# First expert layer on tokens sorted by expert, with rows gathered by index and outputs gathered back per token

## The chip, the cores and the metric

The kernel is one program on one core of a Trainium2 chip. The metric is device time in microseconds of one execution, the median of a few runs. The engines are PE (TensorE; PEld is its weight load), DVE (VectorE), ACT (ScalarE), POOL (GpSimd) and SP (SyncE, which issues the transfers of the kernel before; SPq is its queue).

## What is computed

Four layers follow each other on x, 8 batches of 256 tokens with 128 features. Each layer is a cross-attention and a feed-forward part, both on the layer-normed x and both added to x. The feed-forward part of the first layer is a channel mix; those of the other three are mixtures of eight experts. The change is in the second layer's, `moe1` in the kernel:

```python
logits = xf @ router_w.T                       # xf: 2048 tokens x 128, eight experts
routing = softmax(logits)
top_w, top_i = top_k(routing, 2); top_w = top_w / sum(top_w)
combine = zeros(N, E).at[arange(N)[:, None], top_i].add(top_w)
g = einsum('nd,ehd->neh', xf, w_gate)          # hidden size 256
u = einsum('nd,ehd->neh', xf, w_up)
y = einsum('neh,edh->ned', silu(g) * u, w_down)
out = einsum('ned,ne->nd', y, combine)
```

Only two of eight entries of a row of `combine` are not zero.

## The kernel before, in words

x stays in SBUF as `x_sb`, 16 tiles of 128 tokens by 128 features. The program is written out per engine; engines meet through semaphores that count named events. `EVENTS` lists them; `wait` and `done` turn a stage, block and step into a count. Each engine runs its own list in order.

The stages are, in order, `att0` with `ffn0` and `att1` (one flow of 16 steps), `moe1`, `att2`, `moe2`, `att3`, `moe3`. An attention flow goes in steps of one batch, and each step in beats of one head; in a step, the scores' rows of one batch (maxima on DVE, L712), the exponentials of the batch before (ACT, L1256) and the output of the batch before that are interleaved. After the last batch come steps with `tail` 0 to 3, in which less and less is left of the attention; the statistics, norms and transposes (`stats_all`, `apply_all`, `turn_all`) of the next stage stand there, at fixed beats.

In `moe1` each of four blocks of 512 tokens goes through each of eight experts (`block_of`, `down`, `add_y`). For one block and one expert PE makes four products of 512 columns from the transposed tokens `zt` (gate and up, two halves of the hidden size each, L1810). A float32 product is two passes on PE. ACT takes Silu of the gate (`gated`, L1407), DVE multiplies it by up (`ht`, L971). PE then makes eight products of 128 columns with the down weights (L1778), and DVE adds each of the four 128-token results to `x_sb` with the router's weight as a scalar (`add_y`, L950); the weight is zero for six of eight experts. Blocks 1 and 2 are a loop with a register; blocks 0 and 3 are written out. Beside block 0 the router runs on DVE (`route_logits`, `route_pick`, `route_weights`). Beside the last block the first step of the next attention, `att2`, runs (`beside_last_block`, `EARLY_BEATS`). The router looks at its tokens in two groups, `GROUPS`, of 12 and 4 tiles.

All weights of the layer are one transfer into `pack_moe`, made at the start. `stack` are three buffers that hold the attention's keys and queries, split into bf16 parts; `scratch` is a DRAM table that `moe3` uses. Nothing in the kernel before is addressed by data, and POOL issues no transfer.

## Time and profile before

| | |
|---|---|
| three runs, median (lowest to highest) | 907.48 us (905.09 to 909.58) |
| profiled execution, its own time | 905.37 us |
| its span, from the first to the last instruction | 903.6 us |
| mean granted TensorE clock | 0.96 |
| instructions | 14923 |
| DMA moved | 44.52 MB |

The span is what the profile shows; 1.8 us of the profiled execution's time lie around it. Times of rows are microseconds from the start of the span unless marked ns. PEclk in a window is the granted clock of TensorE as a share of full speed: 1.00 is 2.4 GHz, 0.50 is 1.2 GHz.

### The profile page before, as it was taken

Reading aid. Unit: us, or ns where it says so; the run is one execution under the profiler, and the core shown is the slowest. Engines: PE = TensorE matmul, PEld = TensorE weight load, DVE = VectorE, ACT = ScalarE, POOL = GpSimd, SP = SyncE. Lnnn points to the kernel's source line nnn. Section 1 sums busy time; section 2 is a strip of 40 time slices with the busy share of each in tenths; the row PEclk is TensorE's granted clock in tenths of the full one; section 3 lists DMA queues with packets and bytes.
Section 4 is the critical chain, followed back from the end, with each engine's and each line's share of the span. In section 5 each row is a group of like instructions: output and inputs, shape, how many; then the busy total and the mean of one; then the engine's idle time right before and its main releaser. Section 6 shows DMA issues by size and latency. Waiting matters only on the chain. (4 is left out here: it accounts for less than half of the span.)

```text
span 903.6 us, 14923 instructions
## 1 busy us (share of the span) xinstructions
PE 787.9 (87%) x5120; PEld 533.7 (59%) x5120; DVE 513.8 (57%) x1423; ACT 391.6 (43%) x764; POOL 174.6 (19%) x316
## 2 busy tenths in 40 slices
PE   1687888999988899999997897789999887769998
PEld 1355666666655566666665565467777666546665
DVE  4577768767775374444556775484235434445453
ACT  2565554566667532222222665453333455232221
POOL 4444455333301000000013442200001001000000
PEclk9999999999999999999997999899999999569999
DMA  9422212321110000000014331000000200023332
GB/s 308 115 69 66 71 55 61 88 68 55 55 55 2 1 1 1 1 0 0 1 36 138 89 84 38 1 1 1 1 0 1 79 1 1 1 72 95 94 95 68
DMA packets 55277, 44.52 MB, mean 49 GB/s; under 512 B 5048, under 2 KB 50104, under 8 KB 54728
## 3 DMA queue, kind: packets, MB, share of 16 engines
q1 hardware_dynamic: 55208, 43.63, 16.5%
q8 instruction: 39, 0.64, 0.3%
q14 instruction: 30, 0.25, 0.1%
HBM read 20.09 MB, written 1.11 MB: 23 GB/s over the span
## 5 line engine op out<-in xcount | busy, mean ns | idle before, releaser
L712 DVE TENSOR_REDUCE negmax<-ps 128x2 f32<-128x512 f32 x256 | 170.0, 687 | 88.2 <-PE ps L1539 87.2
L1256 ACT ACTIVATE exps<-ps 128x512 f32<-128x512 f32 x256 | 148.2, 598 | 79.8 <-PE ps L1551 78.3
L1810 PE MATMUL ps<-zt,pack_moe 128*128 128x512 f32 (+1 forms) x384 | 177.5, 598 | 0.9 <-DVE ht L971 0.9
L1778 PEld LDWEIGHTS ps<-pack_moe,ht 128*128 128x128 f32 x1024 | 124.0, 192 | 30.7 <-issue 28.8
L1778 PE MATMUL ps<-pack_moe,ht 128*128 128x128 f32 x1024 | 124.6, 275 | 0.5 <-ACT ht L1410 0.5
L950 DVE SCALAR_TENSOR_TENSOR x_sb<-ps,weights,x_sb 128x128 f32<-128x128 f32 (+1 forms) x256 | 72.1, 344 | 79.7 <-PE ps L1778 79.5
L1539 PE MATMUL ps<-stack 96*128 96x256 bf16 x512 | 100.4, 290 | 19.2 <-DVE negmax L712 14.1
L1551 PE MATMUL ps<-stack 99*128 99x256 bf16 x512 | 98.1, 281 | 14.9 <-DMA stack<-maxt 10.1
L1810 PEld LDWEIGHTS ps<-zt,pack_moe 128*128 128x128 f32 x384 | 68.9, 193 | 63.7 <-issue 62.1
L1407 ACT ACTIVATE gated<-ps 128x512 f32<-128x512 f32 x64 | 38.1, 597 | 117.1 <-PE ps L1810 117.0
L971 DVE TENSOR_TENSOR ht<-ps,gated 128x512 f32<-128x512 f32 x64 | 44.0, 691 | 57.9 <-ACT gated L1407 57.8
L1551 PEld LDWEIGHTS ps<-stack 99*128 99x128 bf16 x512 | 43.4, 100 | 54.1 <-DMA stack<-maxt 20.4
L1539 PEld LDWEIGHTS ps<-stack 96*128 96x128 bf16 x512 | 47.2, 101 | 41.7 <-DVE negmax L712 28.1
L1567 PE MATMUL ps<-exps,values 128*32 128x256 f32 x1024 | 69.8, 388 | 0.5 <-ACT exps L1256 0.5
L1410 ACT ACTIVATE ht<-ps,pack_moe 128x512 f32<-128x512 f32 x64 | 43.2, 686 | 57.6 <-PE ps L1810 56.3
L1425 ACT ACTIVATE gated<-ps 128x512 f32<-128x512 f32 x36 | 21.5, 597 | 77.5 <-PE ps L1842 77.4
L1853 PEld LDWEIGHTS ps<-pack_moe,ht 128*128 128x128 f32 x288 | 37.6, 193 | 19.8 <-issue 13.5
L940 DVE TENSOR_TENSOR ht<-ps,gated 128x512 f32<-128x512 f32 x36 | 24.9, 691 | 39.6 <-ACT gated L1425 39.5
L1069 POOL TENSOR_SCALAR var_eps<-moments 128x2 f32<-128x2 f32 x24 | 4.7, 197 | 208.1 <-DVE moments L594 202.7
L1853 PE MATMUL ps<-pack_moe,ht 128*128 128x128 f32 x288 | 38.7, 277 | 2.7 <-DVE ht L940 2.7
L1567 PEld LDWEIGHTS ps<-exps,values 128*32 128x32 f32 x1024 | 28.7, 110 | 19.4 <-issue 6.4
L1840 PE MATMUL ps<-stack,pack_moe 128*128 128x512 f32 x64 | 33.9, 611 | 5.3 <-DVE stack L1010 5.3
(183 smaller groups left out, 1053.8 us busy)
## 6 DMA issues: line engine op xcount, KB each, us to landing
stack<-qk_parts SPq DMA_DIRECT2D x168, 128.0 KB
stack<-weights_t SPq DMA_DIRECT2D x32, 256.0 KB, 3.2
pack_moe<-in_moe SPq DMA_DIRECT2D x1, 3076.0 KB, 14.6
pack_moe<-in_moe SPq DMA_DIRECT2D x1, 2129.0 KB, 9.6
pack_moe<-in_moe SPq DMA_DIRECT2D x1, 1732.0 KB, 7.0
out<-x_sb SPq DMA_DIRECT2D x4, 256.0 KB, 2.3
x_sb<-in_x SPq DMA_DIRECT2D x1, 896.0 KB, 6.0
ctxt_sb<-in_ctxt SPq DMA_DIRECT2D x1, 768.0 KB, 8.0
```

The lines of the kernel that those rows point to most:

```text
L712: dve.tensor_reduce(negmax_of[b % 2][:, :, h:h + 1].rearrange("p t h -> p (t h)"), ps[:, h % 2, :].rearrange("p (t k) -> p t k", t=2), AX, ...
L950: last = dve.scalar_tensor_tensor(out=xt, in0=ps[:, 4 + e % 2, t * D:(t + 1) * D], scalar=w, in1=xt, op0=ALU.mult, op1=ALU.add)
L971: dve.tensor_tensor(ht[:, e % 2, c, :], ps[:, 2 * c + 1, :], gated[:, c, :], ALU.mult)\
L1256: nc.scalar.activation(exps[:, i, :], ps[:, 2 + h % 2, :], ACT.Exp, scale=scale)\
L1407: nc.scalar.activation(gated[:, c, :], ps[:, 2 * c, :], ACT.Silu).then_inc(sem["gate_done"], 1)
L1410: nc.scalar.activation(ht[:, e % 2, c, :], ps[:, 2 * (e % 2) + c, :], ACT.Gelu, bias=par(s, "b1")[:, k:k + 1]).then_inc(sem["h_ready"], 1)
L1539: last = pe.matmul(ps[:, h % 2, t * T:(t + 1) * T], st[0:MAXROW, h, 0, t * P:(t + 1) * P], st[0:MAXROW, h, 1, :], start=True, stop=True)
L1551: last = pe.matmul(ps[:, 2 + h % 2, t * T:(t + 1) * T], st[0:MAXROW + 3, h, 1, t * P:(t + 1) * P], st[0:MAXROW + 3, h, 0, :], start=True, ...
L1567: last = pe.matmul(ps[STRIP * k:STRIP * (k + 1), AV, r * T:(r + 1) * T], values[nh][:, buf(s, a), kt, u, :], exps[:, slot(s, a, u), kt * T ...
L1778: last = pe.matmul(ps[:, 4 + e % 2, t * D:(t + 1) * D], ht[:, e % 2, c, t * P:(t + 1) * P], par(s, "wd" if s == "moe1" else "w2")[:, k * P ...
L1810: last = pe.matmul(ps[:, bank, :], par(s, name)[:, k * P:(k + 1) * P], zt[:, bass.ds(2 * blk, 2), 1:1 + T], start=True, stop=True)
L1853: last = pe.matmul(ps[:, 4 + blk % 2, t * D:(t + 1) * D], ht[:, q % 2, 0, t * P:(t + 1) * P], par(s, "w2")[:, w * P:(w + 1) * P], start=(q ...
```

## The change

The tokens are taken in two halves of 1024 (`HALVES`). In each half the two picks of every token are put in order of expert, each expert's rows padded up to whole tiles of 128. 8 experts and 2048 rows need at most 23 tiles (`TILES`), so 46 tiles are always computed (`ALL_TILES`). The steps for one half:

- The normed rows go to a DRAM table (`store_table`, on SP).
- `rank_tokens` (PE) counts, with triangular and all-ones matrices, how many picks of each expert stand ahead of each token. `place_tokens` (DVE) makes the row of each pick from it. `make_lists` (DVE) writes one-hot matrices, `list_tokens` (PE) multiplies them into the token number of each row, and `read_tokens` (DVE) makes integers of them. `make_lists` also makes the expert of each tile as an offset into the weights.
- POOL gathers 128 rows per tile by indirect DMA (`fetch_rows`), six tiles ahead (`AHEAD`).
- PE turns the rows, multiplies them by gate and up weights at the offset read into a register (one product of 512 columns with the rows as weights), turns the hidden values (two transposes) and multiplies them by the down weights. ACT copies the turned rows and hidden values out of PSUM and takes Silu; DVE multiplies, and copies the output to `y_kept`.
- SP stores each output tile to DRAM (`store_output`).
- POOL fetches, for each token tile, the rows of its two picks (`fetch_output`), and DVE adds them to `x_sb` with the shares as scalars (`join_outputs`).

The first half's routing stands in the steps `tail` -1 to 2 of `att1` (`SORT_STEPS`), the second half's beside the tiles 1 to 20 (`SORT_BEATS`). The first half's outputs are fetched from loop step 26 on, the second half's in the steps of `att2`. The first batch of `att2` runs beside tiles 33 to 45 (`EARLY_TILES`).

```diff
-    "moe1": [("router", 8), ("wg", 2048), ("wu", 2048), ("wd", 2048)],
+    "moe1": [("router", 8), ("experts", 6144)],
+TOKENS = 1024
+PARTS = 2
+TILES = E + (2 * TOKENS - E) // P
+ALL_TILES = PARTS * TILES
+AHEAD = 6
+KEPT = 4
+BACK = 16
+SORT_STEPS = {"stats": (-1, 5), "rstd": (-1, 9), "norm": (-1, 12), "turn": (1, 3), "turned": (1, 4), "logits": (1, 5),
+              "top": (1, 6), "exp": (1, 7), "first": (1, 8), "second": (1, 10), "weigh": (1, 12), "rank": (1, 15),
+              "place": (2, 2), "list": (2, 4), "listed": (2, 6)}
+EARLY_TILES = (33, 34, 36, 37, 39, 41, 43, 45)
+JOIN_TILE = {"fetch": 26, "join": 30}
...
+            def fetch_rows(s, j):
+                g, i, landed = j // TILES, *ring(s, j, AHEAD)
+                if j % TILES == 0:
+                    pool.wait_ge(table_out, 16 * (SORTED.index(s) * PARTS + g + 1))
+                    wait(pool, "tokens_ready", s, 0, g)
+                if j >= AHEAD:
+                    wait(pool, "taken_psum", s, 0, j - AHEAD)
+                at = bass.IndirectOffsetOnAxis(ap=tokens[:, g, j % TILES:j % TILES + 1], axis=0)
+                pool.indirect_dma_start(taken[:, i, :], None, table[s, g], at).then_inc(taken_in[i], 16)
+            def fetch_output(s, t, k):
+                g, i = t // (NT // 2), t % (NT // 2)
+                if i == 0 and k == 0:
+                    wait_outputs(pool, s, g)
...
+                at = bass.IndirectOffsetOnAxis(ap=placed[:, g, k * NT // 2 + i:k * NT // 2 + i + 1], axis=0)
+                pool.indirect_dma_start(back[:, n, :], None, averaged[s, g], at).then_inc(back_in[n], 16)
...
+            def join_outputs(s, t):
+                g, i = t // (NT // 2), t % (NT // 2)
+                for k in range(2):
+                    n, landed = fetched(s, t, k)
+                    dve.wait_ge(back_in[n], landed)
+                    at = k * NT // 2 + i
+                    last = dve.scalar_tensor_tensor(out=x_sb[:, t, :], in0=back[:, n, :], scalar=share[:, g, at:at + 1],
+                                                    in1=x_sb[:, t, :], op0=ALU.mult, op1=ALU.add)
...
+            def sorted_tiles(s):
+                weights_at = {}
+                for j in range(-2, ALL_TILES + 2):
+                    if 0 <= j + 2 < ALL_TILES:
+                        i, landed = ring(s, j + 2, AHEAD)
+                        pe.wait_ge(taken_in[i], landed)
+                        pe.wait_ge(sem["taken_ready"], done("taken_ready", s, 0, j + 1)) if j >= -1 else None
+                        pe.transpose(ps[:, 2, 0:P], taken[:, i, :], ident).then_inc(sem["taken_psum"], 1)
+                    if 0 <= j + 1 < ALL_TILES:
+                        if (j + 1) % TILES == 0:
+                            g = (j + 1) // TILES
+                            pe.wait_ge(sem["experts_ready"], done("experts_ready", s, 0, g))
+                            found = nc.values_load_multi_w_load_instructions(
+                                expert_at[0:1, g, :], [mybir.EngineType.PE], min_val=0, max_val=(E - 1) * EXPERT[s],
...
+                        pe.wait_ge(sem["taken_ready"], done("taken_ready", s, 0, j + 1))
+                        pe.wait_ge(sem["h_ready"], done("h_ready", s, 0, j - 1)) if j >= 1 else None
+                        at = weights_at[j + 1]
+                        pe.matmul(ps[:, (j + 1) % 2, :], taken_t[:, (j + 1) % 2, :], par(s, "experts")[:, bass.ds(at, 2 * T)],
+                                  start=True, stop=True).then_inc(sem["up_psum"], 1)
+                    if 0 <= j < ALL_TILES:
+                        pe.wait_ge(sem["h_ready"], done("h_ready", s, 0, j))
+                        pe.wait_ge(sem["ht_ready"], done("ht_ready", s, 0, j - 1)) if j >= 1 else None
+                        for c in range(2):
+                            last = pe.transpose(ps[:, 3, c * P:(c + 1) * P], hidden[:, j % 2, c * P:(c + 1) * P], ident)
+                        last.then_inc(sem["ht_psum"], 1)
+                    if 0 <= j - 1 < ALL_TILES:
+                        pe.wait_ge(sem["ht_ready"], done("ht_ready", s, 0, j - 1))
...
```

Three places show how the instructions of an engine stand, before and now. The first is PE in `moe1`: before, two rows are one expert of one block (`zt` the transposed tokens, `pack_moe` the weights, `ht` the hidden values), of which two are shown.

```order
L1810 MATMUL ps<-zt,pack_moe 128x512 x4
L1778 MATMUL ps<-pack_moe,ht 128x128 x8
L1810 MATMUL ps<-zt,pack_moe 128x512 x4
L1778 MATMUL ps<-pack_moe,ht 128x128 x8
```

Now one tile of the loop reads so; `ht` holds the gathered rows (L2223) and the hidden values (L2241, L2248), `gated` the turned rows, and an ISA row sets an address.

```order
L2223 MATMUL ps<-pack_consts,ht 128x128
L2235 ISA
L2235 MATMUL ps<-pack_moe,gated 128x512
L2241 MATMUL ps<-pack_consts,ht 128x128 x2
L2248 ISA
L2248 MATMUL ps<-pack_moe,ht 128x128
L2248 ISA
L2248 MATMUL ps<-pack_moe,ht 128x128
```

A tile has one product of 512 columns, two of 128 and three transposes, where a block's expert had four and eight.

The second place is DVE at the end of `att1`. Before, the last output of the attention follows the norms of the next stage at once.

```order
L637 TENSOR_SCALAR z<-x_sb,moments,rstd 128x128 x12
L671 TENSOR_TENSOR x_sb<-ps,xb 128x256
L658 RECIPROCAL rden<-ps 128x32
L661 TENSOR_TENSOR o<-ps,rden 128x256
L671 TENSOR_TENSOR x_sb<-ps,xb 128x256
```

Now 13 steps of placing (the last one is shown) and the lists stand between the residual of the seventh batch and the reciprocal (L794) of the eighth.

```order
L1117 SCALAR_TENSOR_TENSOR row<-row,place 128x16
L1130 TENSOR_TENSOR stack<-row,pack_consts 128x1024
L1133 TENSOR_TENSOR stack<-row,pack_consts 128x368
L1130 TENSOR_TENSOR stack<-row,pack_consts 128x1024
L1138 TENSOR_TENSOR stack<-stack,pack_consts 128x736
L1143 TENSOR_TENSOR full<-full 128x8
L1144 TENSOR_TENSOR stack<-full,pack_consts 128x184
L1147 TENSOR_REDUCE stack<-stack 128x23
L1148 TENSOR_SCALAR expert_at<-stack 128x23
L1156 TENSOR_SCALAR stack<-ps 128x23
L1157 TENSOR_TENSOR tokens<-ps,stack 128x23
L794 RECIPROCAL rden<-ps 128x32
```

The norms have moved ahead, into the last full step of `att1`, eight tiles of them for this stage.

The third place is POOL in the second half of the tile loop, where before it had nothing but one batch's statistics. `table_moe_1` is the second half's table, `outputs_moe_0` the first half's outputs, `late` the buffer for fetched rows.

```order
L1486 DMA ht<-table_moe_1,tokens 128x128 x9
L1498 DMA late<-outputs_moe_0,placed 128x128
L1486 DMA ht<-table_moe_1,tokens 128x128
L1498 DMA late<-outputs_moe_0,placed 128x128
L1486 DMA ht<-table_moe_1,tokens 128x128
L1498 DMA late<-outputs_moe_0,placed 128x128
```

From there to the end of the loop a fetch follows each gather. In each of four steps of `att2`, four fetches stand ahead of the splitting of the maxima (L1394 is L1091 of before):

```order
L1446 TENSOR_TENSOR qk_parts<-qk_rest,qk_parts 128x2x256
L1498 DMA late<-outputs_moe_1,placed 128x128 x4
L1394 CAST negmax_parts<-negmax 128x2x8
```

Before, the cast followed the first of these rows directly.

## Rows read from the trace of the kernel before

**Rows 1.** The page's busy times of the engines.

```profile
PE 787.9 (87%) x5120; PEld 533.7 (59%) x5120; DVE 513.8 (57%) x1423; ACT 391.6 (43%) x764; POOL 174.6 (19%) x316
```

**Rows 2.** Windows: stretch, length, busy time by engine, clock, DMA share, GB/s.

```profile
225.00:250.00 25.00, 22.92 (x224) 15.72 (x226) 17.76 (x33) 16.79 (x37) 9.69 (x17) 1.00 0.18 53
304.80:345.00 40.20, 39.26 (x188) 25.49 (x188) 27.09 (x91) 15.67 (x22) 1.21 (x2) 0.99 0.00 1
sum 175.80, PE 173.62 PEld 111.72 DVE 95.28 ACT 47.14 POOL 6.01; mean PE 34.72 PEld 22.34 DVE 19.06 ACT 9.43 POOL 1.20
```

**Rows 3.** Timeline around start and end of the layer: start, length, engine, instruction.

```profile
295.15 0.61 PE L1551 MATMUL ps<-stack 99*128 99x256 bf16 x4
...
304.76 4.18 PE L1810 MATMUL ps<-zt,pack_moe 128*128 128x512 f32 x8
...
308.78 2.74 PE L1475 MATMUL ps<-pack_moe,zt 128*128 128x8 f32 x24
...
480.62 0.67 PE L1605 MATMUL ps<-zt,pack_att 128*128 128x256 f32 x2 [1.26 <-issue]
```

**Rows 4.** Timeline of one expert of one block, in the steady layer.

```profile
428.68 3.60 PE L1810 MATMUL ps<-zt,pack_moe 128*128 x8
...
432.12 1.95 PE L1778 MATMUL ps<-pack_moe,ht 128*128 128x128 f32 x16
...
433.90 3.60 PE L1810 MATMUL ps<-zt,pack_moe 128*128 128x512 f32 x8
```

**Rows 5.** Groups by line: busy us, mean ns, idle before.

```profile
L971 DVE TENSOR_TENSOR ht<-ps,gated 128x512 f32<-128x512 f32 x64 | 44.0, 691 | 57.9 <-ACT gated L1407 57.8
L1407 ACT ACTIVATE gated<-ps 128x512 f32<-128x512 f32 x64 | 38.1, 597 | 117.1 <-PE ps L1810 117.0
L1137 POOL TENSOR_TENSOR qk_rest<-qk,qk_parts 128x512 f32<-128x512 f32 x24 | 27.8, 1157 | 40.2 <-DVE qk_parts L723 40.2
L602 DVE TENSOR_SCALAR z<-x_sb,moments,rstd 128x128 f32<-128x128 f32 x48 | 21.5, 566 | 1.8 <-POOL rstd L1075 1.8
L637 DVE TENSOR_SCALAR z<-x_sb,moments,rstd 128x128 f32<-128x128 f32 x64 | 17.7, 350 | 11.3 <-issue 7.0 <-POOL rstd L1059 4.3
L1270 ACT ACTIVATE ot<-ps 128x256 f32<-128x256 f32 x24 | 9.4, 392 | 3.4 <-PE ps L1521 3.4
L671 DVE TENSOR_TENSOR x_sb<-ps,xb 128x256 f32<-128x256 f32 x16 | 6.7, 418 | 15.4 <-PE ps L1662 8.9 <-PE ps L1528 6.5
L1407 ACT ACT_TABLE_LOAD x3 | 3.8, 1283 | 4.5 <-PE ps L1810 4.5
```

**Rows 6.** Timeline of two small router steps on DVE.

```profile
313.58 0.26 DVE L887 TENSOR_TENSOR rt<-lg,rs 128x96 f32<-128x96 f32 x1
313.88 0.26 DVE L888 TENSOR_TENSOR rt<-rt,pack_consts 128x96 f32<-128x96 f32 x1
```

**Rows 7.** Transfers: issues in the timeline, and the page's time to landing.

```profile
491.58 0.76 SPq L532 DMA_DIRECT2D stack<-maxt  x1
793.32 0.30 SPq L541 DMA_DIRECT2D weights_t<-wt  x1
795.44 20.90 SPq L561 DMA_DIRECT2D stack<-weights_t  x8
out<-x_sb SPq DMA_DIRECT2D x4, 256.0 KB, 2.3
```

**Rows 8.** Timeline of POOL in one step of the attention after.

```profile
496.32 1.15 POOL L1143 TENSOR_TENSOR qk_parts<-qk_rest,qk_parts 128x512 bf16<-128x512 f32 x1
500.25 0.20 POOL L1091 CAST negmax_parts<-negmax 128x16 bf16<-128x16 f32 x1 [2.77 <-DVE negmax L712]
```

**Rows 9.** Windows with the granted clock (third number from the end).

```profile
299.00:303.00 4.00, 1.65 (x7) 0.99 (x7) 0.77 (x2) 1.22 (x3) 0.00 (x0) 0.94 0.00 0
303.00:305.00 2.00, 2.00 (x9) 2.00 (x10) 0.00 (x0) 0.00 (x0) 0.00 (x0) 0.50 0.00 0
...
740.00:750.00 10.00, 8.40 (x54) 6.72 (x52) 3.74 (x13) 5.20 (x18) 0.64 (x1) 1.00 0.00 1
```

550 lines of the change are left out of this document (445 added, 105 removed).

## The prediction

> **What bounds the kernel now.** I read the page's totals first: the TensorE is busy for 87% of the span and no other engine reaches 60% [rows 1]. Then the windows over the first expert layer, from its first product at 304.76 to the first product of the next attention at 480.62 [rows 2, 3]: 175.9 us, TensorE busy in 173.6 of 175.8, granted clock 0.99 in its first quarter, DMA idle. So the layer costs what its products cost. The timeline of one steady expert of one block gives the price [rows 4]: eight passes of the up products (four products of 512 columns, two passes each) from 428.68 to 432.12, 0.43 us a pass; sixteen passes of the down products (128 columns) from 432.12 to 433.90, 0.111 us a pass. That is 5.22 us for one expert and 512 tokens, 32 times: 167 us. Every token passes through all eight experts although the router keeps two. Silu (597 ns) and the product on the VectorE (691) lie beside it [rows 5].
>
> **What the change does to this sum.** The 8 x 4 blocks of 512 tokens go, and 46 tiles of 128 rows come. A tile holds rows of one expert, up to 23 tiles for a half of 1024 tokens. By the order above its TensorE work is one transpose of the gathered rows, one product of 512 columns (gate and up together; two passes), two transposes of the hidden values and two down products (four passes of 128 columns). With the pass prices: 2 x 0.43 + 7 x 0.111 = 1.64 us, the three transposes taken at the price of a down pass, since they too stream 128 columns. 46 x 1.64 = 75.4 us in place of 167.
>
> Can the others follow at 1.64? ScalarE per tile: a copy of 128 columns, Silu on 256, a copy of 256. 512 columns take 597 ns and 256 take 392 [rows 5], so 128 take some 290: 1.07 us. VectorE: a product of 256 columns 0.42 [rows 5] and a copy of 128 at some 0.28: 0.70 us. The ring from an up product over Silu and product back to the transposes: 0.39 + 0.42 and three handovers of 0.1 to 0.2, about 1.3 us, against the 1.6 us of other TensorE work between them. It fits, with little to spare, so I add 0.1 us a tile for waits: 4.6 us.
>
> What comes on top inside the layer:
> - TensorE work of sorting and of the next attention's first batch: 8 transposes 0.9; 16 router products 1.8 (24 took 2.74 [rows 3]); about 25 small products for ranks and lists at 0.1, 2.5; the early batch some 1.8, as before. Together 7.
> - One read of 23 weight offsets into TensorE registers at the start of each half. No row shows such a read; the bounds are 0.26 (a small router step [rows 6]) and some 2.3 us, the landing of a transfer [rows 7], and it may scale with the count. I take 2 and 1: 3.
> - Two activation table loads of 1.28 [rows 5] for the exponential of the second half's router, now beside a ScalarE that is two thirds full: 2.6. Lumps of sorting work on the VectorE (two equality tests of 1024 columns, by the slope of 128x256 to 128x512 [rows 5] some 1.24 us each, against 0.9 us of slack a tile): 2.
> - The handover between the halves. The second token list is read at tile 20; then an issue and a landing (2.3 [rows 7]) must pass before tile 23's rows can be turned, one tile later in the program: 4.
> - The end of the pipeline, two tiles deep: 2.
>
> **GpSimd is the open price.** It issues 46 gathers and 16 fetches of 128 rows beside the tiles and 16 more fetches in the next attention. Before has no indirect DMA and no DMA issued by GpSimd. Nearest rows: SyncE issues transfers in 0.30 to 0.76 us [rows 7], and once eight of them take 20.90, 2.6 each, where they also wait. GpSimd needs 1157 ns for what the VectorE does in 691 [rows 5], 1.67 times. I take the longer single issue times this ratio: 0.76 x 1.67 = 1.27 us, ends 0.30 and 2.6. At 1.27 a gather hides under a tile of 1.74. But from loop step 26 on each step has a gather and a fetch (the order above): 2.54 us against some 2.0 (tile and early batch), over 15 tiles 8 us, of which the six tiles gathered ahead absorb some 3: 5 us.
> The Trainium skill, "DMA: Bandwidth & Descriptors", Latency and other measured facts, puts the first byte of a GpSimd-issued DMA at about 1 us, from descriptor emission. If that were the whole issue time, the estimate from that page would be 2 us a pair and this 5 us term would be nothing; no run here shows it yet.
>
> Outside the layer:
> - Start. The lists of the first half are made in the last steps of the attention before. Rank products go out near 290.5; the VectorE then has 13 small steps at 0.26 to 0.29 each [rows 6] and four wide ones (2 x 1.24, 0.93, 0.53), 7.3 us, so the lists stand near 299. The TensorE asks for them where it stood at 295.15 before [rows 3], waits some 4 us, spends 1.5 on 16 list products, and what followed (295.15 to 304.55) moves with it: 5 us. The VectorE was nearly idle there, so the steps themselves cost nothing more; the first gathers land during that tail.
> - The statistics and norms of the first eight tiles (some 2.4 and 2.3 us) move from an idle VectorE to one that is busy 17.76 of 25 us and which the TensorE waits on [rows 2]: 3.
> - Next attention. One GpSimd step of it has 2.77 us idle between its last cast of keys (ends 497.47) and the maxima at 500.25, and it is the maxima's splitting that lets the row go out [rows 8]. Four fetches at 1.27 are 5.1 us: the maxima start up to 2.3 us late in four steps. Some of it is slack; the joins add 1.4 us a step to the VectorE. 4 in all.
> - The clock. It stands at 0.50, the 1.2 GHz level, in the window from 303, after the TensorE was busy 1.65 of 4 us [rows 9]; a pass takes twice as long there. Two new waits of about 4 us, at the lists and at the handover, I price at 2 us each: 4.
>
> **Sum.** Layer after: 75.4 + 4.6 + 7 + 3 + 4.6 + 4 + 2 + 5 = 105.6. Outside: 5 + 3 + 4 + 4 = 16. Less 175.9: a change of -54.3. The profiled execution took 905.37, the runs' median is 907.48: 851 from the one, 853 from the other. I say 852.
>
> **Rivals.**
> 1. GpSimd sets the pace somewhat: an indirect issue of 1.6 to 2.1 us. The single stretch then runs at the issue time, the double one at twice that. With r for the issue time the layer is 62r + 12, and the next attention loses 4 x (4r - 2.8). At r = 1.8: 123.6 + 17.6 + 12 (start, statistics, clock) - 175.9 = -22.7, so 883. For it: nobody else issues, and 78 issues depend on it. Against: the 1.27 above.
> 2. Slower than before, one mechanism: the issue itself. 62r + 12 + 16r - 11 + 12 passes 175.9 at r = 2.1. At the upper end, 2.6, it is +40: 945. For it: 2.6 per issue has a row. Against: those issues also waited for their semaphores. The Trainium skill, "SBUF — State Buffer", SBUF: two separate sides, gives a way to get there: descriptors are written through a port pair that the VectorE can lock with single-source SBUF operations. In rows: norms of SBUF tiles average 566 ns beside a working GpSimd and 350 elsewhere [rows 5], so something is shared; but in the tile loop such operations are eight norms and some copies, a few us in 90, and the rest read PSUM or two tensors. That is why I hold it unlikely.
> 3. The clock stays low over the tiles, since three of nine passes are transposes. A tile is then 3.3 us, 76 us more for 46: 928. Against: the third attention has many transposes and gaps and is granted 1.00 at 84% busy [rows 9]. The layer before also starts at the lower level and is at 0.99 over its first 40 us [rows 2].
> 4. All goes better: issue below 0.9 us, no waits per tile (4.6), pairs hidden (5), next attention untouched (4), clock terms nil (4), register reads short (2): 852 - 20 = 832.
> 5. The sorted layer is as long as the dense one for reasons of waits between engines at each tile (3.6 us a tile instead of 1.74): no change. Every tile crosses engines six times, but two are in flight, so little.
>
> **Numbers.** Forecast, 838 to 868: 0.55. Better than that (4): 0.10. Rival 1, 868 to 902: 0.20. Same: 0.02. Rival 2: 0.08. Rival 3 and its like: 0.05. What a measurement of this kernel tells from no change is about 0.5%, 4.5 us. Faster 0.85, same 0.02, slower 0.13. Range 828 to 902, where the low end takes the lowest bounds and the high end an issue near 2.0; it leaves out a little under 2 in 10.
>
> **What the profile after would show.** Right: the layer near 106 us, TensorE some 85% busy in it, tiles 1.7 to 1.9 us apart in the first half and 2.0 to 2.6 where fetches start; a TensorE wait of 4 us on the lists before the last projections and one at tile 23 on the gather; GpSimd issues 1.0 to 1.5 us apart when nothing holds them. Wrong: tiles apart by exactly the issue time (rivals 1, 2), a clock of 0.50 over the tiles (3), tiles waiting on Silu or the VectorE product at full clock (5), or steps of the next attention longer than 10 us with the maxima waiting behind fetches.

## The result, and the profile after

The changed kernel takes 881.7 us (median of 4 runs, 879.73 to 886.63) against 908.31 of the kernel before (4 runs): a ratio of 0.972, 95% interval 0.967 to 0.977. That is 26.6 us less. Forecast were 852 us, 55 less. So the sign was right and the time lies inside the full range (828 to 902), but it is outside the forecast's own band, 838 to 868, in that of rival 1, and the gain is 0.48 of what was forecast.

The profiled execution took 879.73 us, with a span of 877.9. Before it was 905.37 with 903.6, so the two traces differ by 25.7 us. The page's busy times, for [rows 1]:

```profile
PE 722.3 (82%) x4816; PEld 487.6 (56%) x4816; DVE 491.9 (56%) x1409; ACT 397.3 (45%) x837; POOL 250.5 (29%) x394
```

TensorE is busy 66 us less, but the span shrinks by 26 only: TensorE idles 40 us more than before, and a part of the busy time runs at the lower clock. Where, the windows tell (stretch, length, busy time by engine, granted clock third from the end). Their bounds are marks of the timeline: 304, inside the wait for the lists, the first tile's product (gate and up, L2235) at 323.0, tile 21's product at 366.7, tile 25's at 386.8, tile 33's at 399.8, the next attention's first product at 437.6, the first product of the layer after it at 557.4.

```profile
304.00:323.00 19.00, 9.74 (x54) 5.58 (x54) 7.71 (x29) 4.04 (x8) 6.15 (x7) 0.51 0.09 21
323.00:366.70 43.70, 41.37 (x228) 26.52 (x229) 26.74 (x93) 22.99 (x66) 17.95 (x19) 0.94 0.27 65
366.70:386.80 20.10, 11.71 (x40) 7.13 (x39) 3.12 (x11) 5.98 (x13) 8.52 (x9) 0.75 0.19 44
386.80:399.80 13.00, 13.00 (x74) 8.78 (x73) 5.37 (x18) 7.37 (x24) 7.91 (x9) 1.00 0.29 78
399.80:437.60 37.80, 28.72 (x140) 17.80 (x138) 18.01 (x59) 14.09 (x44) 25.78 (x29) 1.00 0.28 67
437.60:557.40 119.80, 87.40 (x688) 54.92 (x689) 74.58 (x189) 56.16 (x120) 58.16 (x92) 0.86 0.32 82
```

The fourth row is the kernel as it was meant to run: eight tiles in 13.0 us, TensorE never idle, full clock. Each tile there is 1.63 to 1.64 us long (the products of two tiles in the timeline):

```profile
390.03 1.02 PE L2235 MATMUL ps<-pack_moe,gated 128*128 x2
391.67 1.02 PE L2235 MATMUL ps<-pack_moe,gated 128*128 x2
```

The other rows are what it costs to get there and away. Four marks give the balance against the forecast's sum (before: the layer's first product 304.76, the next attention's 480.62 [rows 3], the next layer's 584.33).

| part | before | after | change | forecast |
|---|---|---|---|---|
| first product of the layer | 304.76 | 323.03 | +18.3 | +10 (start 5, statistics 3, clock 2) |
| layer, to the next attention's first product | 175.9 | 114.6 | -61.3 | -68.3 (105.6 and 2 for the clock) |
| next attention, to the next layer's first product | 103.7 | 119.8 | +16.1 | +4 |
| the rest | | | +1.2 | 0 |
| sum | | | -25.7 | -54.3 |

The marks at the start need care. The first product of L2017 (L1631 before), ahead of all sorting, stands at 187.56, and at 184.52 before: 3.0 us of the 18.3 are there already. Most of them arise in the first 60 us of the span, no run shows why, and later traces of the same changed kernel are 6.6 to 7.3 us late at this mark (e5, e9, e13). From it to the product of the same line for the seventh batch, 294.96 against 288.85, 3.1 us come on top, where statistics, norms and router are new; statistics and norms were forecast at 3. Another 2.0 us, the gap ahead of 323.03, are the first register read, which the forecast has in the layer.

**The start.** TensorE's timeline (start, length, in brackets the idle time before and who ended it):

```profile
300.61 0.39 PE L1937 MATMUL ps<-stack 99*128 99x256 bf16 x2
307.16 0.79 PE L2211 MATMUL ps<-stack 128*128 128x46 bf16 x16 [6.16 <-DVE stack L1138]
307.78 0.60 PE L1937 MATMUL ps<-stack 99*128 99x256 bf16 x2
309.06 1.93 PE L1953 MATMUL ps<-exps,values 128*32 128x256 f32 x16 [0.69 <-ACT exps L1618]
...
317.75 2.08 PE L2048 MATMUL ps<-pack_att,hid 128*128 128x128 f32 x8 [0.93 <-ACT hid L1638]
319.62 0.42 PE L2223 MATMUL ps<-pack_consts,ht 128*128 128x128 f32 x1
```

TensorE stands 6.16 us for the lists, and what follows runs at the 1.2 GHz level: L1953 takes 1.93 us here and 1.07 at 299.60. The VectorE makes the lists in 7.7 us, but starts late:

```profile
299.03 0.42 DVE L807 TENSOR_TENSOR x_sb<-ps,xb 128x256 f32<-128x256 f32 x1 [3.33 <-PE ps L2048]
299.37 0.21 DVE L1101 TENSOR_TENSOR stack<-ps,pack_consts 128x64 f32<-128x64 f32 x1
...
306.18 0.92 DVE L1138 TENSOR_TENSOR stack<-stack,pack_consts 128x736 bf16<-128x736 bf16 x1
```

The rank products were done at 296.5 (L2199). The VectorE's first step on them stands in its program behind the residual sum of the seventh batch (L807), and that waits for TensorE.

**The handover.** TensorE again, and the read of the weight offsets into its registers (the query by line; it is listed there and not in the timeline):

```profile
372.47 0.33 PE L2223 MATMUL ps<-pack_consts,ht 128*128 128x128 f32 x1 [4.04 <-DMA ht<-table_moe,tokens]
...
380.56 2.07 PE L2235 MATMUL ps<-pack_moe,gated 128*128 x2 [4.35 <-issue]
```

```profile
L2228 PEldq TENSOR_LOAD <-expert_at x2: 2283/3886/5488, 320.6 to 374.7; - x2
```

Two reads, of 2.28 and 5.49 us. The second makes the 4.35 us gap marked "issue". From tile 21's product to tile 25's pass 20.0 us, where four tiles of 1.64 would be 6.6.

**GpSimd.** It issues a gather or a fetch every 1.25 us:

```profile
413.33 0.95 POOL L1498 DMA_INDIRECT late<-outputs_moe,placed  x1 [0.30 <-issue]
414.58 0.95 POOL L1486 DMA_INDIRECT ht<-table_moe,tokens  x1 [0.30 <-issue]
415.84 0.95 POOL L1498 DMA_INDIRECT late<-outputs_moe,placed  x1 [0.30 <-issue]
```

So a pair takes 2.51 us. The twelve tiles from 399.8 to 432.8 take 2.75 us each, and most of TensorE's waits there end with the landing of gathered rows. The longest does not. GpSimd makes the early batch's statistics (`rstd`) behind its last fetches, the VectorE's norms wait for them, and TensorE waits for what the VectorE does next:

```profile
429.32 1.85 DVE L738 TENSOR_SCALAR z<-x_sb,moments,rstd 128x128 f32<-128x128 f32 x2 [4.16 <-POOL rstd L1377]
```

```profile
431.90 0.44 PE L2241 MATMUL ps<-pack_consts,ht 128*128 128x128 f32 x2 [2.04 <-DVE ht L1220]
```

**The next attention.** Its first rows come late, and then its steps take 13.2 to 14.1 us while fetches are in them, and 10.3 once they have ended (from one L1841 to the next: 450.10, 463.49, 476.73, 489.93, 504.07, 514.42). TensorE at the first step, and GpSimd in the second, for [rows 8]:

```profile
443.90 1.03 PE L1925 MATMUL ps<-stack 96*128 96x256 bf16 x4 [5.19 <-DMA stack<-qk_parts]
```

```profile
447.55 1.15 POOL L1446 TENSOR_TENSOR qk_parts<-qk_rest,qk_parts 128x512 bf16<-128x512 f32 x1
448.87 1.13 POOL L1498 DMA_INDIRECT late<-outputs_moe,placed  x1 [0.16 <-issue]
...
452.80 0.95 POOL L1498 DMA_INDIRECT late<-outputs_moe,placed  x1 [0.30 <-issue]
453.76 0.20 POOL L1394 CAST negmax_parts<-negmax 128x16 bf16<-128x16 f32 x1
```

Four fetches stand between the keys' last cast and the splitting of the maxima, 448.7 to 453.8, where GpSimd waited 2.77 us before.

### The profile page after: what moved, and what is told of

It is laid out like the page before. It is cut to its first block and busy times, and to the rows that moved or that the text cites. A ratio compares the mean times of both kernels' runs of the same rounds, so it can differ in the third digit from the quotient of the medians.

```text
span 877.9 us, 14680 instructions
## 1 busy us (share of the span) xinstructions
PE 722.3 (82%) x4816; PEld 487.6 (56%) x4816; DVE 491.9 (56%) x1409; ACT 397.3 (45%) x837; POOL 250.5 (29%) x394
## 3 DMA queue, kind: packets, MB, share of 16 engines
q1 hardware_dynamic: 63912, 47.88, 19.3%
## 5 line engine op out<-in xcount | busy, mean ns | idle before, releaser
L1937 PE MATMUL ps<-stack 99*128 99x256 bf16 x512 | 98.9, 283 | 16.4 <-DMA stack<-maxt 13.7
L1953 PE MATMUL ps<-exps,values 128*32 128x256 f32 x1024 | 72.1, 399 | 0.7 <-ACT exps L1618 0.7
L2174 PEld LDWEIGHTS ps<-pack_moe,ht 128*128 128x128 f32 x512 | 62.3, 193 | 16.4 <-issue 14.6
L1267 DVE SCALAR_TENSOR_TENSOR x_sb<-ps,weights,x_sb 128x128 f32<-128x128 f32 (+1 forms) x128 | 36.1, 344 | 61.8 <-PE ps L2174 61.6
L2174 PE MATMUL ps<-pack_moe,ht 128*128 128x128 f32 x512 | 62.6, 275 | 0.5 <-ACT ht L1796 0.5
L2269 PE MATMUL ps<-zt,pack_moe 128*128 128x512 f32 (+1 forms) x128 | 62.1, 608 | 0.0
L1486 POOL DMA_INDIRECT ht<-table_moe,tokens x46 | 44.4, 965 | 50.5 <-DVE tokens L1157 22.7
L2235 PE MATMUL ps<-pack_moe,gated 128*128 x92 | 53.5, 665 | 6.4 <-issue 6.4
L1809 ACT ACTIVATE gated<-ps 128x512 f32<-128x512 f32 x36 | 21.5, 598 | 77.3 <-PE ps L2298 77.3
L2309 PEld LDWEIGHTS ps<-pack_moe,ht 128*128 128x128 f32 x288 | 37.9, 194 | 19.8 <-issue 13.5
L1257 DVE TENSOR_TENSOR ht<-ps,gated 128x512 f32<-128x512 f32 x36 | 24.9, 692 | 39.8 <-ACT gated L1809 39.8
L1220 DVE TENSOR_TENSOR ht<-ps,gated 128x256 f32<-128x256 f32 x46 | 19.5, 423 | 49.0 <-ACT gated L1774 33.8
L2309 PE MATMUL ps<-pack_moe,ht 128*128 128x128 f32 x288 | 39.0, 279 | 2.7 <-DVE ht L1257 2.7
L1440 POOL TENSOR_TENSOR qk_rest<-qk,qk_parts 128x512 f32<-128x512 f32 x24 | 27.8, 1157 | 46.9 <-DVE qk_parts L859 46.9
L1953 PEld LDWEIGHTS ps<-exps,values 128*32 128x32 f32 x1024 | 29.6, 112 | 20.3 <-issue 7.3
## 6 DMA issues: line engine op xcount, KB each, us to landing
pack_moe<-in_moe SPq DMA_DIRECT2D x1, 2129.0 KB, 10.1
```

The source lines that it names most:

```text
L1267: last = dve.scalar_tensor_tensor(out=xt, in0=ps[:, 4 + e % 2, t * D:(t + 1) * D], scalar=w, in1=xt, op0=ALU.mult, op1=ALU.add)
L1486: pool.indirect_dma_start(taken[:, i, :], None, table[s, g], at).then_inc(taken_in[i], 16)
L1937: last = pe.matmul(ps[:, 2 + h % 2, t * T:(t + 1) * T], st[0:MAXROW + 3, h, 1, t * P:(t + 1) * P], st[0:MAXROW + 3, h, 0, :], start=True, ...
L1953: last = pe.matmul(ps[STRIP * k:STRIP * (k + 1), AV, r * T:(r + 1) * T], values[nh][:, buf(s, a), kt, u, :], exps[:, slot(s, a, u), kt * T ...
L2174: last = pe.matmul(ps[:, 4 + e % 2, t * D:(t + 1) * D], ht[:, e % 2, c, t * P:(t + 1) * P], par(s, "w2")[:, k * P:(k + 1) * P], start=(c = ...
L2235: pe.matmul(ps[:, (j + 1) % 2, :], taken_t[:, (j + 1) % 2, :], par(s, "experts")[:, bass.ds(at, 2 * T)], start=True, stop=True).then_inc(s ...
```

## The experiments

The runs came in five groups, each on one chip, and are compared inside a group. In three of them (e5 to e8, e13 to e16, e17 and e18) the unchanged kernel took 880.1, 878.9 and 880.5 us. In one (e9 to e12) it took 899.8, beside 907.6 for the kernel before, with stops over the tiles that are told with e9; e1 to e4, the first group, have the same stops and no unchanged kernel beside them. Their medians are therefore read against e9, and their effects from marks in their traces. The record gives the chip of e1 to e4 and that of e13 to e16 the same number, 0, with stops in the first group and none in the other, so the stops do not go with that number. "From the last tile's product to the next layer" below is from the start of the last tile's down product (L2248) to the next layer's first product; it is 121.0 us in the first profile and 120.2 to 120.3 in e5, e13 and e18.

**e1: maxima first, fetches behind.**

```
+ for st, b, _ in due(flow, (tail, heads), u, "m", max_chain("split")):
+     split_max(st, b)
  ... four fetch_output(...)
- for st, b, _ in due(flow, (tail, heads), u, "m", max_chain("split")):
-     split_max(st, b)
```

> The changed kernel with one thing moved: in the attention after the layer, GpSimd splits the maxima first and issues its four fetches behind them. Theory A (the four fetches, 5.0 us ahead of the splitting, stretch four steps from 10.3 to 13.2 us each): with 10.7 us of GpSimd work left in a step, the steps fall to 10.7 to 11.2 us, so 8 to 10 us less, 871 to 874. Theory B (the two joins of 0.73 us a step on the VectorE and the landing of the fetched rows stretch the steps): the steps stay near 13 us, 879 to 883.

Measured: 897.7 us (896.8 to 899.4), ratio to before 0.988 [0.984, 0.992]. The first step, which holds the wait for the first rows, takes 14.4 us, the four with fetches 13.8, 13.8, 13.5 and 13.5; from the last tile's product to the next layer 121.6 us, as in e9 (121.6). Nothing gained. GpSimd's timeline shows why:

```profile
481.75 0.20 POOL L1394 CAST negmax_parts<-negmax 128x16 bf16<-128x16 f32 x1 [2.92 <-DVE negmax L848]
...
482.98 1.08 POOL L1498 DMA_INDIRECT late<-outputs_moe,placed  x1 [0.16 <-issue]
...
488.16 0.80 POOL L1377 TENSOR_TENSOR rstd<-var_eps,neghalf 128x2 f32<-128x2 f32 x1
488.95 1.15 POOL L1440 TENSOR_TENSOR qk_rest<-qk,qk_parts 128x512 f32<-128x512 f32 x1
```

The 2.9 us idle place before the maxima is back, but the casting of the next keys (L1440) now has none before it: it comes 5 us of fetches later, and the rows made from it too. The block moved from one place of a ring to the other.

**e2: the first batch's rows ahead of the last four stores** in SyncE's queue.

```
- for j in range(ALL_TILES):
+ for j in range(ALL_TILES - KEPT):
  ...
  if (s, p) == EARLY:
+     for j in range(ALL_TILES - KEPT, ALL_TILES):
+         store_output("moe1", j)
```

> The changed kernel with one thing moved: SyncE sends the rows of the next attention's first batch ahead of the last four stores of tile outputs, not behind them. Theory A (the 5.19 us that TensorE waits for those rows at 438.7 comes from their place in SyncE's queue): the wait goes, 4 to 5 us less, 876 to 878. Theory B (the maxima, the weight load of the next layer or the fetches hold the first steps anyway): within 1.5 us of the changed kernel.

Measured: 894.8 us (894.4 to 898.2), ratio 0.985 [0.981, 0.990]. The first rows' products start 0.9 us after the attention's first product, not 6.3; but to the next layer pass 120.4 us against 121.6 in e9. The wait is SyncE's queue, as theory A has it; the first step falls from 14.3 us to 9.2, but most of that is taken by the four steps behind it (14.4, 13.7, 15.0 and 14.7 us, where e9 has 13.4, 14.0, 13.2 and 14.1).

**e3: the first half's sort moved.**

```
- "place": (2, 2), "list": (2, 4), "listed": (2, 6)}
+ "place": (2, 1), "list": (2, 10), "listed": (2, 8)}
```

> The changed kernel with the sort of the first half moved at its end: its VectorE block stands ahead of the residual sum of the seventh batch and not behind it, and the list products on TensorE stand after the last batch's products and transposes instead of before them. Theory A (the first tile is late, 323.0 against 304.8, because of places in two in-order queues): lists 2.5 to 3 us earlier, no 6.2 us stop of TensorE ahead of them, first tile product at 313 to 317; 6 to 9 us less, 873 to 876. Theory B (the clock alone: TensorE stands at 1.2 GHz from 305 to 328 whatever the order, and the chain of the last batch is as long): 0 to 3 us less.

Measured: 894.5 us (891.2 to 896.8), ratio 0.984 [0.980, 0.989]. From the rank products to the first tile's product pass 21.8 us, against 26.9 in all runs with the old order (but e11, which fills the wait): 5.1 us less. The time of the clock is not saved: L2017 and L2048 still take 2.05 and 2.07 us. Between the two theories, nearer to A.

**e4: the second read of offsets ahead of the wait** for tile 23's rows.

```
+ if j == 21:
+     g = 1
+     pe.wait_ge(sem["experts_ready"], done("experts_ready", s, 0, g))
+     found = nc.values_load_multi_w_load_instructions(expert_at[0:1, g, :], ...)
  if 0 <= j + 2 < ALL_TILES:
      i, landed = ring(s, j + 2, AHEAD)
      pe.wait_ge(taken_in[i], landed)
```

> The changed kernel with the second read of 23 weight offsets into TensorE registers moved ahead of the wait for tile 23's rows. The read took 2.28 us for the first half (GpSimd idle) and 5.49 us for the second (GpSimd issuing gathers every 1.25 us). Theory A (a read is longer while GpSimd issues): here GpSimd is idle, the read takes 2.2 to 2.6 us and lies in the 4.04 us wait; 4.5 to 6 us less, 874 to 877. Theory B (the second read is long for its own reasons, such as its place in the program): it still takes about 5.5 us, of which 4 lie in the wait; 3 to 4 us less.

Measured: 894.1 us (894.0 to 899.4), ratio 0.985 [0.981, 0.990]. From tile 21 to tile 25 15.3 us, against 20.0 in e9: 4.7 us less. The read itself:

```profile
L2222 PEldq TENSOR_LOAD <-expert_at x1: 5687/5687/5687, 372.0 to 372.0; - x1
```

GpSimd's first gather of the half starts at 374.36 here. A read of 2.3 us begun at 372.0 would have ended by then; it took 5.69. Theory A does not hold; e12 settles what does.

**e5: unchanged**, beside e6 to e8.

> The changed kernel once more, without an edit. The first four variants showed four stops of TensorE, ScalarE and VectorE at the same tiles (398 to 402, 404 to 408, 431 to 434 and 436 to 441 us), some 16 us in all, for which the trace names no releaser; in the profile of the changed kernel only one gap of 2 us stands there. Theory A (the stops are the chip's or the day's, not the edits'): they are here too, or in none of this group, and the unchanged kernel takes the same time as the others less their own effect; 892 to 902 where they appear. Theory B (they come from the edits): 880 to 887 again, with no stops.

Measured: 880.1 us (876.5 to 880.4), ratio 0.967 [0.963, 0.971], no stops. This alone does not tell whether the edits or the chip made them; e9 does.

**e6: the second half's lists three tiles earlier.**

```
- "place": (13, 14, 15), "spread": (16, 17, 18), "list": 19, "listed": 20}
+ "place": (10, 11, 12), "spread": (13, 14, 15), "list": 16, "listed": 17}
```

> The changed kernel with the second half's sorting compressed so that its lists stand three tiles earlier (list products at tile 16, read at 17). Theory A (the wait of 4.04 us for tile 23's rows is lost once directly and again as clock, since TensorE then stands at 1.2 GHz until 386): the wait goes and the clock stays at 2.4 GHz over tiles 22 to 26, whose excess was 13.4 us; 6 to 9 us less than the unchanged kernel (the register read stays). Theory B (only the wait goes, the clock falls anyway at the register read of 5.5 us): 3 to 5 us less. Theory C (the denser sorting work on the VectorE delays the tiles beside it by as much): 0 to 2.

Measured: 875.0 us (873.9 to 880.6), ratio 0.965 [0.960, 0.969], 5 less than e5 with intervals that overlap. In the traces the tiles take 106.0 us from first to last product against 109.4. From tile 21 to 25 they gain 5.4, and lose 1.9 over tiles 0 to 21, where the sorting now stands denser. The wait for rows is gone, the clock still falls at the register read:

```profile
378.60 2.07 PE L2235 MATMUL ps<-pack_moe,gated 128*128 x2 [5.01 <-issue]
```

Theory B, with a part of C.

**e7: 12 of the 16 fetches beside the tiles left out**, with their joins (six token tiles get no expert output).

```
+ if 2 <= t < NT // 2:
+     return
  if i == 0 and k == 0:
      wait_outputs(pool, s, g)
```

> The changed kernel without 12 of the 16 fetches that GpSimd makes beside the tiles and without their joins (six of sixteen token tiles get no expert output). Theory A (GpSimd's pairs of a gather and a fetch, 2.51 us a tile, set the pace of the last fifteen tiles, which took 2.4 us and more each): the last tiles come at 1.7 to 2.2 us (the early batch's work stays), 8 to 12 us less than the unchanged kernel. If the stops without a releaser hang on GpSimd's dense issues, they go too, and it is up to 25 less. Theory B (the early batch's work on the VectorE and TensorE sets the pace there): 0 to 4 us less.

Measured: 870.1 us (866.2 to 873.0), ratio 0.958 [0.953, 0.963]: 10 less than e5. First to last product 99.4 us against 109.4, all of it from tile 33 on. The windows over the last stretch of tiles, e7 and then e5:

```profile
395.80:423.30 27.50, 26.65 (x146) 18.05 (x145) 14.80 (x59) 14.99 (x49) 17.58 (x21) 1.00 0.30 71
```

```profile
398.70:436.30 37.60, 29.76 (x146) 18.59 (x145) 17.93 (x59) 15.39 (x49) 29.16 (x33) 1.00 0.29 72
```

The same 146 passes: TensorE is busy for 97% without the twelve fetches, 79% with them. Theory A: the pairs on GpSimd set the pace, and cost 10 us. The waits of 4.16 and 2.04 us shown above are gone here too: the VectorE's norms no longer wait for GpSimd.

**e8: e1, e2, e3 and e6 together.**

> The four moves together on the changed kernel: maxima split ahead of the fetches, the first batch's rows sent ahead of the last four stores, the first half's sort ahead of the residual sum and its list products behind the last batch's, the second half's lists three tiles earlier. If the losses are the separate places in queues that I take them for, they add: 8 to 10, 4 to 5, 6 to 9 and 6 to 9, together 24 to 33 us less than the unchanged kernel of this group. If they hide one another, 10 to 18 less.

Measured: 867.4 us (865.9 to 872.1, 6 runs), ratio 0.956 [0.952, 0.959]: 12.7 less than e5. By marks: start -5.0, tiles -4.1, from the last tile's product to the next layer 115.6 against 120.3, -4.7. Together with the moved fetches the early rows of e2 pay more than alone. The sum lies in the band given for moves that hide one another (10 to 18), not in that for moves that add (24 to 33).

**e9: unchanged again**, beside e10 to e12.

> The changed kernel a third time, as the measure for the three runs beside it. Two chips gave 881.7 and 880.1 us for it; the four first variants took 894 to 898 on another, with stops that no instruction of theirs explains. If this group runs on such a chip, it takes 892 to 898 here and shows the same stops; if not, 878 to 883.

Measured: 899.8 us (897.8 to 904.7, 5 runs), ratio 0.993 [0.991, 0.996]. So the stops are not the edits': the unchanged kernel has them in one group and not in another. By marks they cost 16.6 us: from tile 25 to 33 24.6 us pass, against 13.1 in e13, and from tile 33 to 45 37.8, against 32.7. The copies of tile outputs on the VectorE, and TensorE's products behind them:

```profile
400.63 0.29 DVE L1227 COPY y_kept<-ps 128x128 f32<-128x128 f32 x1 [3.04 <-remote]
407.82 0.29 DVE L1227 COPY y_kept<-ps 128x128 f32<-128x128 f32 x1 [6.15 <-remote]
```

```profile
401.17 0.71 PE L2248 MATMUL ps<-pack_moe,ht 128*128 x4 [2.46 <-issue]
...
408.36 1.21 PE L2248 MATMUL ps<-pack_moe,ht 128*128 x4 [3.87 <-DVE y_kept L1227]
```

In the first profile no such copy waits for anything but TensorE. The copy waits for TensorE's product and for the store that used its buffer four tiles ago. "remote" is a releaser outside the record.

**e10: the fetches in two pairs**, one ahead of the maxima, one behind.

```
- for t in range(2 * b, 2 * b + 2):
+ for t in (2 * b,):
  ... split_max(st, b)
+ for t in (2 * b + 1,):
```

> The changed kernel with GpSimd's four fetches of a step of the next attention in two pairs: one pair ahead of the splitting of the maxima, one behind it. With all four ahead the steps were 13.2 to 14 us, with all four behind 13.5 to 13.8: the block only changed from one wait of GpSimd (2.8 us, for the maxima) to the other (2.3 us, for the keys' first cast). Theory A (GpSimd is a ring of one batch a step, with two idle places of 2.3 and 2.8 us, and 5.0 us of fetches in one of them leaves 2.5 us or so over): in pairs of 2.5 us they fit, the steps fall to 10.4 to 11.2, and 8 to 12 us go. Theory B (the joins, 1.5 us a step on the VectorE, and slower maxima beside GpSimd's work stretch the steps): they stay above 12.5, 0 to 4 us less.

Measured: 897.7 us (894.1 to 898.8), ratio 0.988 [0.985, 0.990]. Steps 12.3, 13.8, 12.4, 13.3 us against 13.4, 14.0, 13.2, 14.1 in e9, 2.9 us less in sum, of which 2.0 are left at the next layer (119.6 us from the last tile's product, against 121.6). The time is theory B's (0 to 4 less), the steps are near its bound of 12.5; whether the joins are the cause, as it says, this run does not test.

**e11: idle products in the wait for the lists.**

```
+ if g == 0:
+     for _ in range(8):
+         pe.matmul(ps[:, 0, :], ident, par(s, "experts")[:, 0:512], start=True, stop=True)
  wait(pe, "lists_ready", s, 0, g)
```

> The changed kernel with eight idle products (512 columns, two passes each, some 6.9 us, result overwritten) on TensorE ahead of its wait for the first half's lists; they cover the 6.16 us wait and perhaps 0.7 more. Theory A (the wait costs twice, since TensorE stands at 1.2 GHz from 304 to 328 after it): the clock stays at 2.4 GHz through the last batch's products and the first tiles; 3 to 6 us less. Theory B (what follows the wait is a chain of short steps between engines, in which the clock falls anyway or doesn't matter): within 1.5 us, or up to 1 more.

Measured: 896.6 us (890.0 to 898.5, 6 runs), ratio 0.990 [0.988, 0.992]. From the rank products to the first tile's product 24.5 us against 26.9. Windows of e11, from the wait to the first product, and then of e9 over the like stretch (the clock is the third number from the end):

```profile
304.00:321.00 17.00, 10.87 (x65) 6.07 (x63) 8.03 (x29) 4.04 (x8) 6.25 (x8) 0.82 0.09 24
```

```profile
308.00:327.00 19.00, 10.12 (x55) 5.97 (x56) 7.33 (x28) 4.04 (x8) 6.46 (x8) 0.51 0.08 21
```

L1953, L1975 and L2017 run at 2.4 GHz; by L2048 (2.08 us) the clock has fallen, in the gaps between these short steps. So the clock of this wait is worth 2.4 us; just under theory A's 3 to 6, and above theory B's 1.5.

**e12: e8 with the fetches in pairs and the second row of offsets aligned.**

```
- expert_at = sb("expert_at", [P, PARTS, TILES], I32)
+ expert_at = sb("expert_at", [P, PARTS, 32], I32)
```

> The combined kernel (867.4 us) with the fetches in pairs instead of all behind the splitting, and with the second half's row of weight offsets starting at a multiple of 128 bytes, not at byte 92. If the pairs fit GpSimd's idle places, 8 to 10 us less, 857 to 860. For the read of the offsets (2.3 us in the first half and 5.5 in the second, wherever it stood): if the row's place in memory makes the difference, it takes 2.3 here too and gives 3 us more, 854 to 857; if the second read is long for another reason (46 registers held at once), it stays at 5.5.

Measured: 880.5 us (875.0 to 885.1, 6 runs), ratio 0.970 [0.967, 0.973], 19.3 less than e9, with the stops. The reads:

```profile
L2235 PEldq TENSOR_LOAD <-expert_at x2: 2122/2201/2280, 317.6 to 369.0; - x2
```

Both take 2.1 to 2.3 us. For the second read the place of its row is what changed against e8, where it took 5.58 us: byte 128 of the tile in place of byte 92. Other places were not tried.

**e13: unchanged, beside e14 to e16.**

> The changed kernel again, only as the measure for the runs beside it: 878 to 883 on a chip of the one kind, 896 to 903 on one of the other.

Measured: 878.9 us (2 runs), ratio 0.967 [0.963, 0.971], no stops.

**e14: eight buffers for outputs instead of four.**

```
- KEPT = 4
+ KEPT = 8
+ kept_at = [y_kept[:, i, :] for i in range(4)] + [mix_w[n][:, i, :] for n in ("wk", "wr") for i in range(2)]
```

> The changed kernel with eight buffers for tile outputs on their way to memory, not four (the other four lie where weights of an earlier stage were). Theory A (the stops on some chips are the VectorE waiting for stores that land late, 9 us and more after their issue, while GpSimd's gathers and fetches are under way): on such a chip the stops go, 12 to 18 us less than the kernel beside it; on a chip of the other kind no change, within 1.5 us. Theory B (the stops have another cause, such as code loading, and the copies only show them): no change on either.

Measured: 882.2 us (876.8 to 883.1), ratio 0.969 [0.965, 0.972]. No stops on either kernel here, so it tells nothing of them, only that the ring of four is no bound without them.

**e15: fetches in pairs and one-column joins of the second half** (eight token tiles get next to no expert output).

```
+ cols = slice(0, 1) if g else slice(0, D)
  last = dve.scalar_tensor_tensor(out=x_sb[:, t, cols], in0=back[:, n, cols], ...)
```

> The changed kernel with the fetches in two pairs and the joins of the second half on one column of 128 instead of all (eight of sixteen token tiles get next to no expert output). Theory A (of the 13.5 us of a step 2.3 are the joins' time on the VectorE between the maxima, and 1 to 2 the fetches in one lump): the steps come at 10.4 to 11.2 us, 8 to 12 us less than the unchanged kernel. Theory B (the fetches' 5 us of GpSimd time are the whole of it, however placed): they stay at 12.3 to 13.8, 2 to 4 us less.

Measured: 880.0 us (876.2 to 882.2), ratio 0.967 [0.963, 0.971]. Steps 12.5, 12.3, 13.3, 13.3 us. In e13, unchanged, the same four take 13.3, 13.7, 11.9 and 14.0: 1.5 us less in sum, 1.9 at the next layer (118.4 against 120.3), and nothing in the medians (880.0 against 878.9). Theory A fails, and the thin joins give nothing that the pairs alone had not given in e10; but the experiment took less away than meant. A pair of joins on the VectorE, in e15 with GpSimd beside it, and in e10:

```profile
461.30 1.41 DVE L1167 SCALAR_TENSOR_TENSOR x_sb<-late,share,x_sb 128x1 f32<-128x1 f32 x2
```

```profile
460.87 1.15 POOL L1441 TENSOR_TENSOR qk_rest<-qk,qk_parts 128x512 f32<-128x512 f32 x1 [0.83 <-DVE qk_parts L859]
462.08 0.61 POOL L1445 CAST qk_parts<-qk_rest 128x512 bf16<-128x512 f32 x1
```

```profile
490.79 1.53 DVE L1166 SCALAR_TENSOR_TENSOR x_sb<-late,share,x_sb 128x128 f32<-128x128 f32 x2
494.61 0.73 DVE L1166 SCALAR_TENSOR_TENSOR x_sb<-late,share,x_sb 128x128 f32<-128x128 f32 x2
```

One column takes nearly as long as 128 where GpSimd subtracts and casts keys at the same time: the pair at 461.30 ends at 462.71, with GpSimd's cast (462.69). Later in the step a full pair takes 0.73 and a one-column pair 0.49 (at 465.18). So the number of columns is not what makes the first pair long, and this run left its time in place.

**e16: e12 with eight output buffers.**

> The best version so far (sort of the first half moved, second lists three tiles earlier, first rows ahead of the last stores, fetches in pairs, the offsets' row aligned) with the ring of eight output buffers. If late stores are the stops: 857 to 863 on a chip of either kind, against 880.5 that the version with four took on the slower kind. If not: 878 to 883 on the slower kind, 858 to 863 on the other.

Measured: 861.8 us (857.7 to 864.3, 6 runs), ratio to before 0.947 [0.945, 0.950], 17.1 less than e13 beside it. From tile 21 to tile 25 8.6 us, where e8, with the row at byte 92, took 14.1: 5.5 us less, 3.4 of them the read and the rest the clock that no longer falls behind it. (The eight buffers are new here too; e12, aligned with four buffers, took 10.2, with a wait of 1.09 us for a copy of an output in it.) The product behind the read:

```profile
373.17 1.12 PE L2243 MATMUL ps<-pack_moe,gated 128*128 x2 [1.24 <-ACT gated L1777]
```

From the last tile's product to the next layer it takes 114.3 us, against 120.3 in e13.

**e17 and e18: eight buffers and unchanged, once more.**

> The changed kernel with eight buffers for tile outputs on their way to memory, once more, since its first run stood in a group without stops. Where the unchanged kernel beside it takes 896 or more: theory A (late stores hold the ring of four) 880 to 886 here, and the copies of outputs wait for nothing; theory B (another cause) within 3 us of the unchanged one, with the same stops. Where the unchanged kernel takes about 880: no difference, and the question stays open.

> The changed kernel as the measure for the run beside it: 876 to 883, or 896 to 903 with the stops.

Measured: 882.2 us (881.5 to 886.0), ratio 0.973 [0.966, 0.979], beside 880.5 (2 runs), ratio 0.969 [0.962, 0.977]. Again no stops on either. The question stays open.

## Why the prediction was half right

**Right: the layer's price by passes.** A tile is 1.64 us by the forecast and 1.63 to 1.64 in the trace wherever TensorE waits for nothing. The 0.1 us a tile for waits was not needed there. **Right: GpSimd's issue.** Taken at 1.27 us, it is 0.95 busy and 1.25 from one to the next. Rival 1, which gave 883 at 1.8 us, comes near the measured time by luck: its mechanism is refuted, an issue takes 1.25 and single gathers never set the pace (1.64 us a tile). Rivals 2, 3 and 5 did not happen. The Trainium skill's figure ("DMA: Bandwidth & Descriptors", Latency and other measured facts), some 1 us for GpSimd's emission, agrees with the 0.95; a sum made with it alone would leave out the 0.30 between two.

**Where the sum failed.** Four terms of it were too small, and the wait for the first rows of the next attention had no term at all. Largest first:

1. "Next attention ... 4 in all" was 16.1. The step is "the maxima start up to 2.3 us late in four steps. Some of it is slack." None of it was slack (four times 2.3 are 9.2). The four steps with fetches take 54.0 us in sum, where the same four took 42.5 before: 11.5 us more. e1 shows that it is a ring, not a place: with the fetches behind the maxima the wait stands before the keys. I had looked at one idle time of GpSimd's step and not asked what the engine does next. Pairs gave 2.0 to 2.9 us back in e10 and, with thin joins, 1.5 to 1.9 in e15, so most of the rest is not the lump. That GpSimd is nearly full then, 10.1 and 10.7 us of work in two steps of 12.5 and 12.1, fits e15's timeline (it idles 1.1 to 1.6 us before the maxima and 0.4 to 0.8 before the keys), but no run isolated it, and none left these fetches out. The other part is a wait that I hadn't seen at all: SyncE sends the first batch's rows behind all stores of tile outputs, 5.19 us, which makes the first step 14.4 us against 10.5 before; moved ahead, 1.2 us came back in e2, and 4.7 in e8, with the moved fetches.
2. "Start ... 5", with statistics and clock 10, was 18.3. Of these 3.0 passed ahead of all sorting, unexplained, and 2.0 are the first register read; the statistics and norms come out as sized (3 forecast; 3.1 from mark to mark, the router's products included). So 10.2 stand against 7 for the start and its clock. The lists' own work was sized right (7.3 forecast, 7.7 measured). Wrong was when it begins: "rank products go out near 290.5" was 296.1, when TensorE itself was 6.1 us late, and the VectorE took them up 2.9 us after their end, behind a residual sum that waits for TensorE; the wait for the lists was 6.16 instead of 4. e3 moved the two places in the queues and got 5.1 us back. The clock on this wait was priced at 2 and e11 measured 2.4.
3. The handover, "4", a read of 1 and a clock of 2, 7 together, was 13.5 us over the four tiles' own time. The wait for rows was 4.04, as forecast. The register read was 5.49 instead of 1, and the clock stayed at the lower level until 386. The term mis-sized is the read; e12 and e16 show what made it long, the row's place in memory.
4. GpSimd's pairs, "5 us", 8 with waits and early batch, were 13.3 us over 1.64 a tile in the last twelve tiles. The mechanism was forecast, the size not: e7 puts 12 of the 16 fetches and their joins at 10 us, and its last twelve tiles at 1.88 us each, near the 2.0 of the forecast. Of the 0.87 us between 2.75 and 1.88 a pair's 2.51 explains 0.63. The rest, 2.9 us over the twelve tiles, is near what I left out: GpSimd's own work for the early batch. 1.0 us of it stands between the gathers (408.09 to 409.09 in its timeline). The next statistics come behind its last fetch, at 428.30, and cost TensorE 2.04 us by way of the VectorE's norms, as shown above; e7 has no such wait. GpSimd's work on keys after that, to 432.33, holds no gather up, since the last one went out at 424.76.

Against these stand terms that came out too high: tiles 0 to 21 took 9.3 us more than 1.64 each, at half clock in the first ones included, where waits, sorting, tables and lumps were priced at some 12.

**Open.** Why the unchanged kernel takes some 19 us more in one group than in the others, 16.6 of them in the stops. Every stop has a copy of a tile's output at its head that was free to run but for the store of four tiles ago, or a product whose row the record lacks. Late stores are my reading, argued only: all three times the ring of eight ran (e14, e16, e17), the unchanged kernel beside it had no stops to remove. Where the steps of the next attention lose the 2 to 3 us each that stay with the pairs is open too, since e15 did not take the joins' time away. And so are the 3.0 us ahead of all sorting: the kernel before has one trace, so no run tells whether they are the change's.

## What to carry to other kernels

When slow engines take over issuing, add up all of such an engine's work in one step of the stage it is put into, not the idle time before one instruction: a ring gave back nothing here when the block was moved around in it, and 1.5 to 2.9 us of 11.5 when it was split. For each new list or table ask on which in-order queue its first step stands, and behind what; moving three such places here, with the fetches in pairs, the row of offsets aligned and more output buffers, took the kernel from 878.9 to 861.8 us. A price with no row of its own that stands alone on TensorE's path deserves a wide range: the register read was put at 1, between bounds of 0.26 and 2.3 from the nearest rows, and took 5.5, outside both.
